# A six-layer decoder on one core: the last block's products by column halves, and block 6's third transposes behind a gate tile

## What is computed

```python
x = _layernorm(x + _L1_xattn_ref(x, ctx_4096, Wq, bq, Wk, bk))
x = _layernorm(x + _L1_ffn_ref(x, gate_t, up_t, down_t, gate_s, up_s, down_s))

def _layernorm(x, eps=1e-05):
    m = jnp.mean(x, axis=-1, keepdims=True)
    v = jnp.var(x, axis=-1, keepdims=True)
    return (x - m) / jnp.sqrt(v + eps)

def _L1_ffn_ref(x, gate_t, up_t, down_t, gate_s, up_s, down_s):
    gate_out = x_flat @ (gate_t * gate_s[:, None]).T      # 512 -> 1792
    up_out = x_flat @ (up_t * up_s[:, None]).T
    hidden = jax.nn.silu(gate_out) * up_out
    return hidden @ (down_t * down_s[:, None]).T          # 1792 -> 512
```

## Time and profile before

| | before |
|---|---|
| median of 3 runs | 645.32 us |
| the profiled execution, its own time | 645.23 us |
| its span, first to last instruction | 643.1 us |
| TensorE busy | 632.0 us (98%) |
| VectorE busy | 396.3 us (62%) |
| ScalarE busy | 381.6 us (59%) |

### The profile page before, as it was taken

One profiled execution on the slowest core, in us unless ns is written; L12 is line 12 of the kernel. 1 busy time (PEld: TensorE's weight loads), 2 busy tenths in 40 slices (PEclk: granted clock), 3 DMA queues, 4 the chain that ended last, 5 costly groups with the idle time before them and its releaser, 6 DMA issues.

```text
span 643.1 us, 8521 instructions
## 1 busy us (share of the span) xinstructions
PE 632.0 (98%) x3226; PEld 470.0 (73%) x3226; DVE 396.3 (62%) x633; ACT 381.6 (59%) x527; POOL 65.0 (10%) x116
## 2 busy tenths in 40 slices
PE   9999999999999999999999999999999999999996
PEld 6655555544558888888888888887777888888874
DVE  4798787667988777767667355335655212125467
ACT  2977789976987697576675154223565343316532
POOL 1032142311330000000000000001211000000012
PEclk9999999999999999999999999999999999999999
DMA  7771585512253134233320003056010322100002
GB/s 246 288 243 52 188 268 172 162 52 92 81 152 120 39 110 139 73 104 111 94 83 2 1 1 131 1 216 274 1 33 2 115 77 88 33 1 0 1 33 99
DMA packets 25590, 63.92 MB, mean 99 GB/s; under 512 B 5541, under 2 KB 10725, under 8 KB 24782
## 3 DMA queue, kind: packets, MB, share of 16 engines
q1 hardware_dynamic: 23294, 61.68, 29.4%
q10 hardware_dynamic: 2256, 1.70, 0.8%
HBM read 58.77 MB, written 4.60 MB: 99 GB/s over the span
## 4 chain that ended last, share of the span: by engine, by line
PE 88%; DVE 4%; ACT 4%; DMA 1%; issue 1%; SPq 1%; POOL 0%; POOLq 0%; DVEq 0%; ACTq 0%
PE bank L1043 18%; PE bank L1031 8%; PE bank L1030 8%; PE bank L1032 8%; PE bank L1122 8%; PE bank L1121 8%; PE bank L882 4%; PE bank L802 3%; PE bank L606 3%; PE bank L741 2%; PE bank L1097 1%; DMA codes<-in_c_qkv 1%; PE bank L912 1%; PE bank L926 1%; PE bank L984 1%
## 5 line engine op out<-in xcount | busy, mean ns | idle before, releaser
L1232 ACT ACTIVATE line<-line 128x1024 f32<-128x1024 f32 x87 | 91.4, 1050 | 0.2
L1030 PE MATMUL bank<-xh,wh 128*128 128x512 f32 x224 | 87.5, 391 | 0.0
L1031 PE MATMUL bank<-xl,wh 128*128 128x512 f32 x224 | 87.5, 391 | 0.0
L1032 PE MATMUL bank<-xh,wl 128*128 128x512 f32 x224 | 87.3, 390 | 0.0
L1043 PE MATMUL bank<-wh,xh 128*128 128x512 f32 x192 | 76.1, 396 | 0.2 <-DVE xl L2128 0.2
L1043 PE MATMUL bank<-wh,xl 128*128 128x512 f32 x192 | 74.9, 390 | 0.0
L2211 DVE SCALAR_TENSOR_TENSOR arena<-bank,ff_s,arena 128x512 f32<-128x512 f32 x28 | 21.0, 752 | 72.9 <-PE bank L1122 63.8
L2128 DVE TENSOR_TENSOR xl<-arena,xh 128x1024 fp32r<-128x1024 f32 (+1 forms) x26 | 29.7, 1141 | 35.4 <-ACT xh L1536 35.3
L1121 PE MATMUL bank<-xh,wh 128*128 128x512 f32 x128 | 50.3, 393 | 0.0
L1536 ACT ACTIVATE xh<-arena 128x1024 fp32r<-128x1024 f32 (+1 forms) x26 | 25.6, 991 | 41.3 <-PE bank L1043 34.8
L1122 PE MATMUL bank<-xl,wh 128*128 128x512 f32 x128 | 49.9, 390 | 0.0
(11 more groups left out here) (219 smaller groups left out, 1264.3 us busy)
## 6 DMA issues: line engine op xcount, KB each, us to landing
codes<-in_c_gu SPq DMA_DIRECT2D x14, 512.0 KB, 3.8
scales<-in_s_gu SPq DMA_DIRECT2D x28, 256.0 KB, 4.0
codes<-in_t_gu SPq DMA_DIRECT2D x8, 512.0 KB, 4.2
codes<-in_c_dn SPq DMA_DIRECT2D x7, 512.0 KB, 4.6
scales<-in_s_dn SPq DMA_DIRECT2D x14, 256.0 KB, 3.9
fold<-in_t_dn SPq DMA_DIRECT2D x1, 3584.0 KB, 15.7
codes<-in_c_qkv SPq DMA_DIRECT2D x6, 512.0 KB, 4.8
scales<-in_t_gu SPq DMA_DIRECT2D x6, 512.0 KB, 3.8
```

Source lines behind the costliest of these rows:

```text
L1030: pe.matmul(dst, wh[:, s, c:c + P], xh[:, k, cols], start=(k == 0), stop=False)
L1031: pe.matmul(dst, wh[:, s, c:c + P], xl[:, k, cols], start=False, stop=False)
L1032: last = pe.matmul(dst, wl[:, s, c:c + P], xh[:, k, cols], start=False, stop=(k == KD - 1))
L1232: nc.scalar.activation(below(slot), below(slot), ACT.Prelu, bias=bias, scale=scale, alpha=alpha).then_inc(bent, 1)
```

## The change

Two parts.

1. The last block's closing products run by column halves. The first twelve matmuls cover columns 0 to 255 and gather in the block's own bank as before; twelve more cover columns 256 to 511 and gather in the bank of block 0, which VectorE has emptied by then. VectorE's `last_halves` takes the place of `last_of` for this block: once the low half is whole it scales and adds all 512 columns (the high ones hold the first eight tiles by then), takes the statistics of the low half, then scales, adds and measures the high half's new part, and joins the two statistics in one `bn_aggr`.
2. On TensorE, `x3_T` of block 6 moves from before `t_gate(2, 0)` to behind it. On ScalarE, its copy out moves behind `t_silu(1, 0)`.

```diff
@@ TensorE, the handover
             x_out(NT - 1)
+            t_gate(2, 0)
             x3_T(NT - 2)
-            t_gate(2, 0)
             t_up(2, 0)
@@ TensorE, the end
-            for b in range(NT):
+            for b in range(NT - 1):
                 for j in T_END:
                     if b == 0:
                         t_landed(j)
                     last = t_products(j, b)
+                last.then_inc(t_d_ps, 1)
+            for h in range(2):
+                cols = slice(h * D // 2, (h + 1) * D // 2)
+                if h:
+                    pe.wait_ge(ln_sum, 4 * NT + 1)
+                for j in T_END:
+                    w = t_dn_part(j)[:, cols]
+                    last = down_products(t_d_bank(0 if h else NT - 1)[:, cols], NT - 1, (hidden_part(xh, j), hidden_part(xl, j)), (w, w), h == 1 and j == T_END[0], j == T_END[-1])
                 last.then_inc(t_d_ps, 1)
@@ ScalarE
             norm_tail(4 * NT - 2)
+            t_silu(1, 0)
             x3_T_out(NT - 2)
-            t_silu(1, 0)
             t_silu(2, 0)
@@ VectorE
-            for b in range(NT):
+            def last_halves():
+
+                row, s = x[:, NT - 1, :], (NT - 1) % 2
+                low, high = slice(0, D // 2), slice(D // 2, D)
+                dve.wait_ge(t_d_ps, NT)
+                link(nc.vector.tensor_tensor(rbuf[:, s, :], t_d_bank(NT - 1)[:, :], ds, ALU.mult))
+                link(nc.vector.tensor_tensor(row, row, rbuf[:, s, :], ALU.add))
+                link(nc.vector.bn_stats(st2[:, 0, :], row[:, low]))
+                dve.wait_ge(t_d_ps, NT + 1)
+                link(nc.vector.tensor_tensor(rbuf[:, s, high], t_d_bank(0)[:, high], ds[:, high], ALU.mult))
+                link(nc.vector.tensor_tensor(row[:, high], row[:, high], rbuf[:, s, high], ALU.add))
+                link(nc.vector.bn_stats(st2[:, 1, :], row[:, high]))
+                dve.wait_ge(ln_done, 5 * NT - 2)
+                link(nc.vector.bn_aggr(mv[:, s, :], st2[:, :, :]))
+                nc.vector.tensor_scalar(rstd[:, s, 0:1], mv[:, s, 1:2], LN_EPS, None, ALU.add).then_inc(ln_stats, 1)
+
+            for b in range(NT - 1):
                 last_of(b)
+            last_halves()
```

## The result

The changed kernel takes 646.49 us (median of 20 runs, 645.3 to 647.06) against 645.37 us of the kernel before, run beside it (20 runs, 644.19 to 646.62). The ratio is 1.0015, with a 95% interval of 1.0009 to 1.0022: slower by 1.1 us by the medians and 1.0 us by the ratio. That is within the 0.2% that I took as the bound of no change, though the interval's upper end is just over it, and on the side that was forecast.

A forecast was written before the change was run, and what follows sets the result against it. PE was taken as the bound, busy 632.0 of 643.1 us, with the end on VectorE. +0.92 and +0.13 us on 645.23 us gave 646.28 us, plus 0.09 us for the median: 646.4 us, range 645.6 to 647.0 us.

The forecast's parts named there:

- VectorE's end: Last block on VectorE: 3.49 us of work against 2.40 us, less 0.17 us of wait, +0.92 us.
- its bounds of 0.36 and 0.725 us: 256-column `bn_stats` on VectorE, put at 0.455 us: half a 512-column operation's 0.725 us, or no saving at all.
- PE's end: Last block's twenty-four half products at 0.12 us each: cost nothing, PE 1.5 us ahead of VectorE's need.
- Rival 2: Last block on PE: weight loads set the half products' pace; at 0.227 us each, 647.2 us; chance 0.07.
- The gate tile: PE near 490 us: the moved tile waits for VectorE's `t_hidden(0, 0)`, so the gap stays; +0.13 us together.
- the hop: Handover to PE after the awaited engine's work, near 490 us: 0.05 us; PE starts 0.08 us later than before.
- The exposed first product: First gate product after PE's wait holds PE for 0.34 us, not 0.227 us, its weight load exposed: +0.11 us.
- the transposes: Block 6's transposes on PE, no longer paying for the wait: 0.35 us in place of 0.41 us, -0.06 us.
- Rival 1: PE near 490 us: bank's wait already met, the gate tile fills the 0.60 us gap, 645.7 us; chance 0.06.
- Rival 3: Last block: VectorE free when the low half lands, so the tail gains 0.6 us, 644.8 us; chance 0.04.
- The sum: Whole kernel: +0.92 us at the end and +0.13 us near 490 us, +1.05 us on the profiled execution's 645.23 us.

The follow-up runs named there:

- The halves alone: Kernel before with only TensorE's last-block products split by column halves in their own bank, VectorE's list unchanged: 645.20 us against 645.36 us, ratio 0.9998.
- the early table load: Kernel before with ScalarE's Silu table load moved ahead of its copy of block 7's attention weights: 644.70 us against 645.11 us, ratio 0.9998.
- the gate part alone: Kernel before with only the change's second part, the moves behind `t_gate(2, 0)` and `t_silu(1, 0)`: 645.24 us against 645.11 us, ratio 1.0003.
- The end alone: Kernel before with only the change's first part, the last block by column halves: 645.89 us against 645.11 us, ratio 1.0013.

## Why the prediction was right

- **VectorE's end: +0.92 us forecast, +0.86 to +0.88 us measured.** Its parts: the work between first operation and last `rstd` 3.49 us forecast, 3.52 us measured. A 256-column addition 0.42 us, `bn_stats` of 256 columns 0.43 us, starts 0.46 us apart (0.455 forecast). Taking the price of `bn_stats` from the 256-column additions was right: its bounds of 0.36 and 0.725 us were far off on both sides. The aggregate of two halves took 0.21 us and not 0.18. The start came 0.07 us behind the start of block 6's last operation (636.88 to 636.95), not behind its end, which I had not counted; that is why the total is a little under the forecast.
- **The Trainium skill's cycle table** in "VectorE: DVE Perf Modes", section "The TRN2 errata", would have had +0.61 us; the same section says itself that this row of the table comes out too low. The rows of 0.42 and 0.43 us speak for taking the measured 256-column row. The section's advice on tiles of 512 elements or more agrees with the trace: 256 columns took 0.42 to 0.43 us, where half of 0.69 us is 0.35 us.
- **PE's end: nothing, with 1.5 us in hand.** Measured 0.12 us a product and 1.54 us in hand. Rival 2 (loads setting the pace, 0.19 us or more) is out: the rows of the loads, 0.19 us long, start every 0.12 us at the half products, so they overlap each other. The halves alone cost 0.15 to 0.2 us, when VectorE waits for both.
- **The gate tile: +0.13 us forecast, +0.25 us measured.** The place and the sign were right; the term was half the size. The step that was short is the hop: PE's first instruction came 1.64 us behind the attention output and not 1.46 us, +0.18 us where I had +0.08. I gave the hop 0.05 us from the row of the transposes, and it took 0.15 us (VectorE's end at 490.16, PE at 490.31 us; 490.64 and 490.78 in the gate part alone). The exposed first product came to +0.08 us (0.31 us) where I had +0.11, the transposes to -0.05 us (0.36 us) where I had -0.06, and 0.04 us lie in the tiles up to block 7's transposes. Block 7's norm ended at 494.73 us, well ahead of them, so nothing was late behind the move.
- **Rival 1** (the gate tile fills the gap) fell in the changed kernel and in the part alone, and the early table load shows what it would have needed. **Rival 3** (the tail gains) fell for the reason named, VectorE's work on block 6; with that work left out a gain of 0.15 us appears, while I had 0.6 us for a free VectorE. There I had let the first pass be over when PE ends. It runs from 635.58 to 637.49 us, and PE's last half product lands at 637.0 us.
- The sum, +1.05 us forecast for the profiled execution, was +1.1 us in its span and +1.12 us in the medians. The forecast's 646.4 us stands beside 646.49 us. That it comes so near is partly luck: the end was put 0.05 us too high and the gate tile 0.12 us too low, and the median of the kernel before is itself anything from 645.11 to 645.37 us, by the set of runs.

## What to carry to other kernels

Before splitting the last tile so that a following engine can start early, read whether that engine is idle at all: here it had 0.17 us of waiting per block, and the split gave it 1.1 us more to do. When work is moved into a gap, look for its own wait: if old and new wait hang on the same earlier event (here a table load), moving that event is what closes the gap. And small edits are best judged by distances inside the trace, once distances that the edit doesn't touch are seen to agree: here 0.1 us could be read, while runs scatter by a microsecond.

## What had not been expected of the hardware

GpSimd's small `tensor_scalar` (L1706) took 0.73 us in the changed kernel, from 637.76 us, where the same operation took 0.26 us for the block before it. It started while VectorE's addition of two SBUF operands ran (637.66 to 638.35 us) and ended at 638.49 us, 0.14 us behind that. The end alone shows the same 0.73 us. In the kernel before it started 0.16 us ahead of the addition. The trace of the kernel before has the same thing elsewhere, beside a VectorE operation of 1,024 columns, again with two SBUF inputs:

```profile
165.79 1.22 DVE L1739 SCALAR_TENSOR_TENSOR line<-line 128x1024 f32<-128x1024 f32 x1
166.10 1.03 POOL L1698 TENSOR_SCALAR rstd<-mv,rstd 128x1 f32<-128x1 f32 x1
```

There it ends at 167.13 us, 0.12 us behind VectorE's operation. The Trainium skill says in "SBUF — State Buffer", section "SBUF: two separate sides", that VectorE and GpSimd share a port pair as an exclusive lock: of a VectorE operation with two SBUF inputs and a GpSimd operation that reads SBUF, the one that starts first has it and the other is blocked. GpSimd's rows agree with this. For VectorE the trace doesn't show it: where GpSimd was first (637.56 to 637.82 us before), the addition from 637.72 us took its usual 0.69 us. ScalarE's norm of block 6 came later by it, ending at 639.33 us, but the half norms that wait for it start at 641.30 us only, so it cost nothing. No run was made for it, and the link is read from these overlaps alone.

Why PE took 0.15 us from VectorE's end to its first product at the gate tile, and 0.05 us at 617.13 us, stays open; it was not tried.
